# Layer 2's state-space stage: both weights of the input spread by TensorE, their sum on GpSimd, the C rows moved by a transfer, the gate of x beside the sines

## The reference

```python
x_path, z = split(x @ W_in.T);  x_path = silu(x_path)
ssm = x_path @ W_x.T                    # 16 B, 16 C, dt_in, lam_in
Bn, Cn = rmsnorm(B + B_bias), rmsnorm(C + C_bias)
dt = softplus(dt_in * W_dt[:, 0] + b_dt);  lam = sigmoid(lam_in)
angles = cumsum(mean(dt)) * softplus(rope_freqs)
Br, Cr = rope(Bn, cos(angles), sin(angles)), rope(Cn, ...)
dA = exp(A * dt);  Bx = Br * x_path;  Bx_prev = Bx one step earlier, 0 at first
u = (1 - lam) * dt * dA * Bx_prev + lam * dt * Bx;  u[0] = dt[0] * Bx[0]
h = dA * h + u;  y = sum(h * Cr over states)
out = ((y + x_path * D) * silu(z)) @ W_out.T
```

## Time and profile before

| | us |
|---|---|
| median of 3 runs | 4925.69 (4912.45 to 4927.64) |
| the profiled execution | 4909.32 |
| its span, first to last instruction | 4907.4 |
| layer 2's state-space stage, first gate of y to the last | 2659.3 to 3171.5 of the span |
| busy in the span: TensorE, VectorE, ScalarE, GpSimd | 3529.0, 3231.1, 2362.5, 2120.6 |
| TensorE's mean granted clock | 0.853 |

### The profile page before, as it was taken

How to read it: one execution, slowest core, us unless ns; L and a number is a source line. 1 busy time by engine, 2 the same in 40 slices (tenths; PEclk the granted TensorE clock), 3 DMA queues, 4 the chain that set the end, 5 groups by cost and what they waited for, 6 DMA issues and landing times. The chain is left out here.

```text
span 4907.4 us, 71549 instructions
## 1 busy us (share of the span) xinstructions
PE 3529.0 (72%) x20958; PEld 2298.0 (47%) x20958; DVE 3231.1 (66%) x6387; ACT 2362.5 (48%) x4454; POOL 2120.6 (43%) x2029
## 2 busy tenths in 40 slices
PE   6867566768884548886448888749974878767686
PEld 4657355723332423333322222236653658745586
DVE  5430772069997267884349899977877766666665
ACT  3334433455651327774235455446753645544345
POOL 0046004649993435553227788721222116401254
PEclk9879777989997769997668898969986879979798
DMA  2011101145551223320223344300000001100012
GB/s 88 21 33 43 44 21 34 43 105 91 93 92 31 81 71 91 93 64 12 58 96 67 67 72 69 66 20 1 1 3 3 0 28 40 66 10 0 34 39 79
DMA packets 223543, 241.36 MB, mean 49 GB/s; under 512 B 38845, under 2 KB 170660, under 8 KB 221460
## 3 DMA queue, kind: packets, MB, share of 16 engines
q1 hardware_dynamic: 200980, 192.20, 17.0%
q0 software_dynamic: 22272, 45.66, 2.9%
HBM read 174.13 MB, written 62.72 MB: 48 GB/s over the span
## 5 line engine op out<-in xcount | busy, mean ns | idle before, releaser
L2452 PE MATMUL s_l_attn_a_y_ps<-XN,c_ident 128*128 128x512 f32 x1024 | 572.1, 670 | 94.6 <-POOL XN L2470 77.1
L2522 DVE TENSOR_TENSOR_SCAN s_l_attn_a_h<-s_l_attn_a_da,XN 128x512 f32<-128x512 f32 x512 | 608.2, 1210 | 22.3 <-POOL XN L2478 15.3
L2460 ACT ACTIVATE s_l_attn_a_da<-s_l_attn_a_delta,s_l_attn_a_a 128x510 f32<-128x510 f32 x512 | 346.0, 685 | 401.1 <-DVE s_l_attn_a_h L2522 398.0
L1086 POOL DMA_INDIRECT XNT<-rows_x,s_l_ffn_ffn_from_row x284 | 277.8, 978 | 464.4 <-DVE s_l_ffn_ffn_to_row L948 379.0
L960 DVE COPY s_l_ffn_ffn_xt<-s_l_ffn_ffn_turned 128x128 f32<-128x128 f32 x284 | 79.7, 291 | 555.9 <-PE s_l_ffn_ffn_turned L1161 244.3
L1091 POOL DMA_INDIRECT rows_y<-PICK,s_l_ffn_ffn_to_row x284 | 296.8, 1045 | 296.4 <-ACT PICK L1032 237.9
L1172 PE MATMUL s_l_ffn_ffn_up<-s_l_ffn_ffn_xt,s_l_ffn_ffn_own_w 128*128 128x128 f32 x2272 | 337.2, 296 | 103.6 <-DVE s_l_ffn_ffn_xt L960 100.7
L4390 DVE TENSOR_REDUCE s_l_attn_b_top<-s_l_attn_b_m_ps 128x2 f32<-128x512 f32 x512 | 330.2, 688 | 83.3 <-PE s_l_attn_b_m_ps L4096 79.4
L1182 PE MATMUL s_l_ffn_ffn_down<-down,s_l_ffn_ffn_hid 128*128 x2272 | 328.5, 291 | 75.6 <-DVE s_l_ffn_ffn_hid L974 47.7
L2452 PEld LDWEIGHTS s_l_attn_a_y_ps<-XN,c_ident 128*128 128x128 f32 x1024 | 185.0, 203 | 420.4 <-POOL XN L2470 292.2
L1172 PEld LDWEIGHTS s_l_ffn_ffn_up<-s_l_ffn_ffn_xt,s_l_ffn_ffn_own_w 128*128 128x128 f32 x2272 | 307.5, 210 | 114.6 <-DVE s_l_ffn_ffn_xt L960 111.6
(11 more groups left out here) (722 smaller groups left out, 8521.2 us busy)
## 6 DMA issues: line engine op xcount, KB each, us to landing
LOG<-s_l_attn_a_c_kept SPq DMA_DIRECT2D x128, 256.0 KB, 4.2
s_l_attn_a_more_c_rows<-s_l_attn_a_c_kept SPq DMA_DIRECT2D x128, 256.0 KB, 4.2
s_l_attn_a_b_rows<-s_l_attn_a_c_kept SPq DMA_DIRECT2D x192, 64.0 KB, 3.5
s_l_attn_b_qr<-s_l_attn_b_q_rows SPq DMA_DIRECT2D x64, 144.0 KB
...
```

The costliest lines, as they stand in the source:

```text
L1086: nc.gpsimd.indirect_dma_start(xin[j % RING], None, k.rows_x[:, :], bass.IndirectOffsetOnAxis(from_row[:, j:j + 1], 0)).then_inc(gathered[ ...
L2452: last = self.nc.tensor.matmul(self.y_ps[:, i, :], self.k.ident[:], self.hc[n % 2][:, i, :], start=(n == 0 and not begun), stop=(n == NST ...
L2460: self.nc.scalar.activation(self.da_half(g, n, i)[:, :, 1:], self.delta[par][:, i, :].rearrange("p (b t) -> p b t", b=BPG)[:, :, 1:], ACT. ...
L2522: self.nc.vector.tensor_tensor_scan(self.h[n % 2][:, i, :], self.da_half(g, n, i).rearrange("p b t -> p (b t)"), self.u[n % 2][:, i, :], 0 ...
```

## The change

For the weights, `rest_row` (-0.5 and 0.5) makes TensorE spread 1 - lam as well, into the second bank of aux, at position 8. VectorE makes raw and ahead from the two banks at position 9, soft at 10 and dx = raw * x at 11; the sum of raw and ahead is made by GpSimd (`sum_parts`, two of 128x512) at 10, between them. The first step of a sequence needs no copy: its lam_in is left out of the tanh, so its weight stays 1. `turn_vt` and `turn_bc` of GpSimd go to 8 and 9. `move_c` is gone: SP's queue moves the C rows from the DRAM copy to cb. `multiply_cb` goes to position 0 of the group itself, sum_cb to 1, correct to 2, sum_delta to 3, cum (`sum_up_delta`) to 4, root to 1. ScalarE's `gate_x(r)` goes to position 7, ahead of the tanh and the sines. project_ssm now waits for lam_read.

```diff
 # SP
         sp.wait_ge(self.c_saved, 16 * (g + 1))
+        if low is not None:
+            rows, rows_landed = low
+            sp.dma_start(rows, self.c_kept[g % 2][NST:2 * NST, :]).then_inc(rows_landed, 16)
...
 # TensorE
             def project_ssm(q):
                 pe.wait_ge(xp_ready, q + 1)
+                since(pe, lam_read, q)
...
             def spread_lam(q):
                 pe.wait_ge(xp_ready, min(q + 2, GROUPS))
                 pe.wait_ge(lam_ready, q + 1)
-                nc.tensor.matmul(aux[:, 0, :], half_row[LAM:LAM + 2, :], lam[LAM:LAM + 2, :], start=True, stop=True).then_inc(lam_up, 1)
-
-            def move_c(q):
...
-                nc.tensor.matmul(aux[0:P - NST, 0, :], k.ident[0:BC, NST:P], bc, start=True, stop=True).then_inc(c_up, 1)
+                pe.wait_ge(cum_ready, q + 1)
+                pe.wait_ge(vt_ready, q + 1)
+                nc.tensor.matmul(aux[:, 0, :], half_row[LAM:LAM + 2, :], lam[LAM:LAM + 2, :], start=True, stop=True)
+                nc.tensor.matmul(aux[:, 1, :], rest_row[LAM:LAM + 2, :], lam[LAM:LAM + 2, :], start=True, stop=True).then_inc(lam_up, 1)
...
 # GpSimd
+            def sum_parts(q):
+                pool.wait_ge(lam_read, q + 1)
+                for i in range(CHH):
+                    last = nc.gpsimd.tensor_tensor(raw[:, i, :], raw[:, i, :], ahead[:, i, :, :].rearrange("p b t -> p (b t)"), ALU.add)
+                last.then_inc(summed, 1)
+
             def between(q, n):
+                if n == 8:
+                    turn_vt(q)
                 if n == 9:
-                    turn_vt(q)
+                    turn_bc(q)
                 if n == 10:
-                    turn_bc(q)
+                    sum_parts(q)
...
 # ScalarE
+            def weigh(q):
+                since(act, lam_up, q)
+                nc.scalar.activation(lam[LAM:F, :].rearrange("p (b t) -> p b t", b=BPG)[:, :, 1:],
+                                     ssm[LAM:F, :].rearrange("p (b t) -> p b t", b=BPG)[:, :, 1:], ACT.Tanh, scale=0.5).then_inc(lam_ready, 1)
...
                     if n == 7 and q < GROUPS:
+                        silu_table()
+                        if r < GROUPS:
+                            gate_x(r)
+                        weigh(q)
                         sines(q)
                         log_table()
                     if n == 10:
-                        nc.scalar.preload_act_table_set("silu_and_others")
-                        if r < GROUPS:
-                            gate_x(r)
+                        silu_table()
                         gate_z(g)
...
 # VectorE
             def split_delta(q):
                 dve.wait_ge(lam_up, q + 1)
-                dve.drain()
-                nc.vector.tensor_tensor(raw[:], delta[q % 2][:], aux[:, 0:1, :].to_broadcast([P, CHH, GROUP]), ALU.mult).then_inc(lam_read, 1)
-                dve.drain()
-                by_seq = [b[:].rearrange("p i (b t) -> p (i b) t", b=BPG) for b in (delta[q % 2], raw)]
-                nc.vector.tensor_tensor(ahead[:].rearrange("p i b t -> p (i b) t")[:, :, 0:SEQ - 1],
-                                        by_seq[0][:, :, 1:SEQ], by_seq[1][:, :, 1:SEQ], ALU.subtract)
-                nc.vector.tensor_copy(by_seq[1][:, :, 0:1], by_seq[0][:, :, 0:1])
-                dve.drain()
+                dve.wait_ge(delta_ready, q + 1)
+                since(dve, dx_ready, q)
+                nc.vector.tensor_tensor(raw[:], delta[q % 2][:], aux[:, 0:1, :].to_broadcast([P, CHH, GROUP]), ALU.mult)
+                rest = aux[:, 1:2, :].rearrange("p a (b t) -> p a b t", b=BPG).to_broadcast([P, CHH, BPG, SEQ])
+                nc.vector.tensor_tensor(ahead[:, :, :, 0:SEQ - 1], delta[q % 2][:].rearrange("p i (b t) -> p i b t", b=BPG)[:, :, :, 1:SEQ],
+                                        rest[:, :, :, 1:SEQ], ALU.mult).then_inc(lam_read, 1)
...
             def make_dx(q):
+                dve.wait_ge(summed, q + 1)
+                nc.vector.tensor_tensor(dx[q % 2][:], raw[:], xp[q % 2][:], ALU.mult).then_inc(scan.dx_made, 1)
...
             def multiply_cb(q):
                 dve.wait_ge(bc_ready, q + 1)
-                dve.wait_ge(c_up, q + 1)
-                nc.vector.tensor_tensor(cb, scan.rest[0:NST, :], aux[0:NST, 0, :], ALU.mult).then_inc(cb_ready, 1)
+                dve.wait_ge(c_moved, 16 * (q + 1))
+                nc.vector.tensor_tensor(cb, cb, scan.rest[0:NST, :], ALU.mult).then_inc(cb_ready, 1)
```

More of the change, by code:

```diff
@@ L3007, in between @@
                     spread_mean(1)
-                    move_c(0)
-                if n == 2 * late:
+                if n == 1 + late:
                     sum_cb(g)
@@ L3159, in sizes @@
                 act.wait_ge(dt_up, q + 1)
-                since(act, dx_ready, q)
+                since(act, scan.dx_made, q)
                 since(act, delta_ready, q)
```

75 lines of the change are left out of this document (40 added, 35 removed).

## The result

The change took 4930.55 us (median of 15 runs, 4919.87 to 4947.39) beside 4923.79 us of the kernel before in the same comparison (15 runs, 4908.28 to 4934.45): ratio 1.0027, with 95% between 1.0016 and 1.0038. The ratio makes it some 13 us slower, the two medians 6.8. Repeated later the ratio was 1.0017 (1.0003 to 1.0032) and the medians lay 10.1 us apart (4925.80 and 4915.67). So the estimates run from 7 to 13 us, and neither interval reaches down to 1: this measurement resolved less than the 0.3% that the prediction allowed it. The forecast of 4930 us held, and so did its case "within 0.3%". Its terms did not all hold, and the ones that missed all missed on the same side: more was lost than they said.

A forecast was written before the change was run, and what follows sets the result against it. The prediction took GpSimd's chain to bound the second half of each group, though VectorE was busiest. Terms -7.7 - 4.5 + 6 + 8.4 + 1 + 1.5 = +4.7 us took the median 4925.7 to 4930 us, range 4906 to 4950.

The forecast's parts named there:

- within 0.3%: Whole kernel: the time stays within about 0.3% (15 us) of the kernel before; chance 0.63.
- Shares and sum: Second half of each group: shares on TensorE and sum on GpSimd shorten GpSimd's chain from 39.6 to 38.4 us; -7.7 us.
- move_c: Position 15 on TensorE: C rows by a transfer remove move_c, 1.5 us less in three low-clock groups; -4.5 us.
- multiply_cb: VectorE, moved from position 15 to 0, where it is never idle: 0.85 us more in 7 groups; +6 us.
- The gate of x: ScalarE at position 7, before the sines: decays of position 8 come 1.4 us later in 6 groups; +8.4 us.
- sum_delta and cum a position later: Moved one position later: count_turns ends 0.15 us after VectorE wants the next decay; +1 us.
- Start: Stage start: longer first spread and later project_ssm(1), against group 0's stall of 5.74 us shrinking by 1.8; +1.5 us.
- the idle 2 us before make_dx: Sign in the profile after: VectorE idle some 2 us before make_dx, released by GpSimd's sum.
- Rival 1: Second half of a group: GpSimd does not bound it, VectorE's own time counts; -23 us, 4903 us; chance 0.17.
- Rival 2: Gate of x at position 7 waits for TensorE at half clock: 23 us more, 4953 us; chance 0.2.
- the forecast's own costs: Bounds of the forecast's own terms: from -15 with -5 to +7 with +6 us, giving 4910 to 4945 us.

## Why the prediction was right

The time came out where it was put, and that was luck: the larger terms were too low, and their errors add up. Step by step:

- **Shares and sum (-7.7 us): wrong.** The step that failed is "the waits of 2.74 and 0.62 go (VectorE is now ahead)", with "the three holds of GpSimd ... become two, for soft and dx, of 1.1 each". Soft was held 6.1 us (7.31 less 1.2), so VectorE was not ahead and GpSimd waited 2.39 and 0.61 us again. The prediction had read such a hold in L3297 ("can only run once GpSimd's products and end are over"), but in the sum it let only VectorE push GpSimd, while GpSimd's run of products, end and two adds held VectorE until GpSimd was empty. Chain 40.4 us in place of 38.4; second halves 43.0 beside 42.5 to 43.5 before, so about nothing gained. With soft elsewhere the chain was 37.3 and the second half 40.0.
- **move_c (-4.5 us): not contradicted.** The two runs with the weights, without and with the rows, lie 6 us apart with intervals that overlap, and no wait for it is left. That "three groups of seven" were at the low clock was luck of one profile: the second profile of before had none, and no wait for move_c either.
- **multiply_cb (+6 us): right in size.** It takes 1.32 us, where it took 0.68 with slack; putting it back took 0.9 us off the first half by the median, 6 us, and 9.3 off all seven, where in two groups the wait at 8 had shrunk as well.
- **The gate of x (+8.4 us): right by itself, too small in the change.** Alone it made 1.37 us of wait, where 1.3 was forecast. In the change the waits at 8 sum to 3.44 + 3 x 2.26 + 2 x 2.67 = 15.6 us, where before had 0.98 in all.
- **sum_delta and cum a position later (+1 us): wrong.** The step said "0.15 late". It looked at ScalarE and not at TensorE, whose positions 3 to 6 became one stretch without a pause and ended 0.75 us later against the angles, just where the gate waits. That is the difference between 2.26 and 1.52, and summed over the waits at 8 of the two runs 4.6 us (15.6 and 10.9). It is shown for all the steps set back together, not for sum_delta alone.
- **Start (+1.5 us): half right.** The stall of 5.74 shrank to 4.13 as said (1.6, forecast 1.8). Not foreseen: in group 0 the spreads stand at 9, as does the split, and at a clock of 0.54 VectorE waited 4.44 us for them.

By the forecast's own signs: ahead took 1.21 us and the two sums 2.47, as said; there was no wait for move_c; the wait at 8 was 2.26 and not 1.3; the idle 2 us before make_dx were not there, but stood as the hold of soft; GpSimd waited 3.6 us (0.62, 2.39 and 0.61) within its chain and was busy for 35.0 us, not 37.

Rival 1 (VectorE bounds the second half) is out by the run with soft late, where VectorE waited and GpSimd did not. Rival 2 (the gate at half clock) did not come: the gate's longer wait was for TensorE at a clock of 1.00. The upper end of the forecast's own costs adds up to 4943, not 4945.

The errors add up to some 15 us more than forecast: 8 from the sum, 4.5 from the steps set later, 2 to 3 from longer waits for the gate in groups 0, 1 and 5. The stage of the first profiles shows 13 of them (17.5 in place of 4.7), the ratio 8 (13 in place of 4.7), the medians only 2 (6.8), and the median of before came out 2 us lower than the one the forecast began from. Why the time shows so much less of the loss than the stage is not explained.

A better kernel came out: weights on TensorE, C rows by a transfer, and the gate, multiply_cb, sum and the other steps where they were. Its two comparisons give 0.9983 and 0.9989 of before, 5 to 8 us less (the second interval reaches 1.0000), and some 15 us less than the change.
